# Rebuilt ends, and attention scores computed one slot ahead of their evacuation, in a top-k attention layer

## What is computed

```python
Q, K, V = proj(Wq, bq), proj(Wk, bk), proj(Wv, bv)        # B, H, L, D = 16, 16, 512, 16
scores = jnp.einsum('bhqd,bhkd->bhqk', Q, K) / math.sqrt(D)
top_vals, _ = jax.lax.top_k(scores, U)                    # U = 31
scores = jnp.where(scores < top_vals[..., -1:], -jnp.inf, scores)
context = softmax(scores) @ V
x = layernorm(x + context @ Wo.T + bo)
x = layernorm(x + (silu(x @ wg.T) * (x @ wu.T)) @ wd.T)
```

## Time and profile before

| | |
|---|---|
| median of 3 runs | 3061.3 us (3058.01 to 3065.76) |
| the profiled execution | 3046.8 us |
| its span | 3045.0 us |
| TensorE busy (PE) | 2680.3 us, 88% |
| VectorE, ScalarE, GpSimd busy (DVE, ACT, POOL) | 2481.3, 2480.9, 2407.2 us |
| granted TensorE clock, mean | 0.951 of 2.4 GHz |
| chain that ended last: PE, DVE, issue, SP's queue, POOL | 36%, 19%, 14%, 11%, 10% |

### The profile page before, as it was taken

How to read it: one execution, slowest core, us unless ns; L and a number is a source line. 1 busy time by engine, 2 the same in 40 slices (tenths; PEclk the granted TensorE clock), 3 DMA queues, 4 the chain that set the end, 5 groups by cost and what they waited for, 6 DMA issues and landing times.

```text
span 3045.0 us, 81353 instructions
## 1 busy us (share of the span) xinstructions
PE 2680.3 (88%) x21045; PEld 1454.1 (48%) x21375; DVE 2481.3 (81%) x12298; ACT 2480.9 (81%) x5894; POOL 2407.2 (79%) x1677
## 2 busy tenths in 40 slices
PE   5889989989998988889989999988989898899985
PEld 2444544545454444444545454444545454454443
DVE  4888888888888878888888888878888888888831
ACT  3788889888888977798888889978879887888931
POOL 1787988888888877788888889877869887888861
PEclk7889999999999999999999999999999999999976
DMA  2211111020111101011020111102011110202000
GB/s 81 48 25 38 28 39 39 25 47 26 41 25 40 39 22 43 18 41 39 25 46 25 43 23 44 36 25 46 26 36 30 34 43 19 47 20 50 2 15 7
DMA packets 91147, 102.67 MB, mean 34 GB/s; under 512 B 34514, under 2 KB 52947, under 8 KB 90579
## 3 DMA queue, kind: packets, MB, share of 16 engines
q1 hardware_dynamic: 88544, 93.73, 12.9%
q10 hardware_dynamic: 2034, 2.76, 0.3%
HBM read 20.86 MB, written 8.39 MB: 10 GB/s over the span
## 4 chain that ended last, share of the span: by engine, by line
PE 36%; DVE 19%; issue 14%; SPq 11%; POOL 10%; ACT 6%; DMA 2%; DVEq 1%; ACTq 0%; POOLq 0%
POOL mask L1070 8%; DVE cand L843 7%; PE bench L679 6%; SPq L349 6%; SPq L348 5%; PE Y_ps L608 5%; PE bench L673 4%; PE ST_ps L623 3%; DVE S L836 3%; PE Y_ps L606 3%; PE ctxT_ps L637 3%; PE bench L549 3%; PE ST_ps L620 2%; PE Y_ps L605 2%; ACT above L467 2%
## 5 line engine op out<-in xcount | busy, mean ns | idle before, releaser
L1070 POOL TENSOR_SCALAR mask<-S,thr,mb 128x512 bf16<-128x512 f32 x1024 | 2119.6, 2083 | 44.1 <-POOL mb L1064 30.0
L843 DVE MAX8 cand<-Y_ps 128x8 f32<-128x128 f32 x4096 | 1072.5, 282 | 5.3 <-issue 5.3
L457 ACT ACTIVATE junk<-S,at_zero,slope 128x512 bf16<-128x512 f32 x1024 | 824.6, 805 | 89.6 <-DVE S L836 89.5
L836 DVE TENSOR_SCALAR_CACHE_REDUCE S<-S_ps,na 128x512 f32<-128x512 f32 x1024 | 756.0, 738 | 163.2 <-PE S_ps L595 145.8
L467 ACT ACTIVATE above<-S,s,steep 128x512 bf16<-128x512 f32 x1024 | 824.5, 805 | 0.6
L475 ACT ACTIVATE PT<-ST_ps 128x512 f32<-128x512 f32 x1024 | 596.7, 583 | 205.7 <-PE ST_ps L623 200.2
L595 PE MATMUL S_ps<-KS,QS 64*128 64x512 f32 x1024 | 520.3, 508 | 4.2 <-DVE S L836 3.6
L608 PE MATMUL Y_ps<-KS,QS 64*128 64x512 f32 x1024 | 520.2, 508 | 0.0
L606 PE MATMUL Y_ps<-above,nbig 128*128 128x512 bf16 x1024 | 398.3, 389 | 85.4 <-DVE cand L843 57.4
L620 PE MATMUL ST_ps<-QS,KS 64*128 64x512 f32 x1024 | 415.4, 406 | 6.2 <-POOL mask L1070 6.2
L623 PEld LDWEIGHTS ST_ps<-nbig,mask 128*128 128x128 bf16 x4096 | 236.7, 99 | 382.5 <-issue 382.5
(11 more groups left out here) (125 smaller groups left out, 3682.1 us busy)
## 6 DMA issues: line engine op xcount, KB each, us to landing
QS<-Qhi SPq DMA_DIRECT2D x512, 32.0 KB, 2.0
KS<-Khi SPq DMA_DIRECT2D x512, 32.0 KB, 2.0
KS<-Klo SPq DMA_DIRECT2D x512, 32.0 KB, 2.0
QS<-Qlo SPq DMA_DIRECT2D x512, 32.0 KB, 2.0
xTs<-in_xT SPq DMA_DIRECT2D x17, 512.0 KB, 3.7
xs<-in_x SPq DMA_DIRECT2D x16, 512.0 KB, 3.9
out<-xs SPq DMA_DIRECT2D x16, 512.0 KB, 3.0
hT<-in_wgT ACTq DMA_DIRECT2D x1, 768.0 KB
```

The costliest lines, as they stand in the source:

```text
L457: nc.scalar.activation(junk[:, :], S[:, score_place(j)[0], :], ACT.Tanh, bias=at_zero[:, :], scale=slope[:, hb, col:col + 1], accum_out=s0 ...
L836: nc.vector.tensor_scalar(S[:, at, :], S_ps[n % 2][:, :], na[:, hb, col:col + 1], None, ALU.add, op1=ALU.max, accum_out=rmax[:, n % RING:n ...
L843: mx = nc.vector.max(cand[:, j % CANDS, i, :], Y_ps[j % 2][:, i * BW:(i + 1) * BW])
L1070: nc.gpsimd.tensor_scalar(mask[:, h % MASKS, t, :], S[:, score_place(j)[0], :], thr[:, r:r + 1], mb[:, r:r + 1], ALU.is_lt, op1=ALU.add).t ...
```

## The change

It has four parts. (1) The start: the network's weights are loaded by SP after the stacks of heads 0 and 1 (five DMAs) instead of by ScalarE's queue at the very start; q, k, keys, gram, quad and sums of the prologue go to six different banks, with semaphores of their own, and wait for fewer loads; ScalarE runs one tiny activation early. (2) TensorE computes the scores of tile T+1 in slot T, still before `turned`; S_ps keeps its two banks, so the wait is now for the evacuation of tile T-1. TensorE's loop holds seven batches (1 to 14) instead of five, and batch 15 stands behind it. (3) In the draining round VectorE makes every second one of the last 17 masks (`late_mask`), POOL the others. (4) The output projection, norms and network of batch 15 leave the draining round and follow it, each step with two banks or more, the copies shared by ScalarE and VectorE, the down-projection interleaved with gate and up over four banks, the last rows normalised on two engines and stored in two halves. The other functions take their bank and semaphores as arguments.

```diff
+LAST_TURN = (GROUP - 16) % TILES
...
-    if not first:
+    if not first and not rest:
...
+            def load_network():
+                sp.dma_start(wo[:, :, :], woT.rearrange("(c p) n -> p c n", p=P)).then_inc(ffn_loaded, 16)
+                sp.dma_start(brow, bo.rearrange("(a n) -> a n", a=1)).then_inc(ffn_loaded, 16)
...
+                sp.dma_start(wd[:, :, :].bitcast(I32), wdT.rearrange("(c p) n -> p c n", p=P)).then_inc(ffn_loaded, 16)
...
+            sp.dma_start(wqk[0][:, :, :], wqT.rearrange("(c p) n -> p c n", p=P)).then_inc(wq_loaded, 16)
+            sp.dma_start(wqk[1][:, :, :], wkT.rearrange("(c p) n -> p c n", p=P)).then_inc(w_loaded, 16)
+            sp.dma_start(wv[:, :, :], wvT.rearrange("(c p) n -> p c n", p=P)).then_inc(late_loaded, 16)
+            sp.dma_start(ranks[:, :], ranks_in).then_inc(late_loaded, 16)
+            sp.dma_start(bvc[:, :], bv).then_inc(late_loaded, 16)
+            sp.wait_ge(first_lo, 2)
             for h in range(HALF):
                 stack(h)
+                if h == 1:
+                    load_network()
...
+            rows = out[B - 1].rearrange("(n p) d -> p n d", p=P)
+            sp.wait_ge(out_done, (B - 1) * NT + 2)
+            sp.dma_start(rows[:, 0:2, :], xs[:, 0:2, :]).then_inc(stored, 16)
+            sp.wait_ge(last_rows, 4)
+            sp.dma_start(rows[:, 2:4, :], xs[:, 2:4, :]).then_inc(stored, 16)
+            sp.wait_ge(stored, 16 * (B + 2))
...
+            for w, src in ((0, bq), (1, bk)):
+                act.dma_start(bqk[w][:, :], src).then_inc(w_loaded, 16)
...
+            act.wait_ge(zero_set, 1)
+            nc.scalar.activation(junk[:, 0:1], at_zero[:, :], ACT.Identity)
             act.wait_ge(w_loaded, 16 * N_W)
...
             slots(0, True, False, False)
...
+            act.wait_ge(last_made, 1)
+            nc.scalar.activation(ctxT[:, :, 0:2 * P].rearrange("p c (n t) -> p n c t", n=2),
+                                 S_ps[0][:, :].rearrange("p (n c t) -> p n c t", n=2, c=C), ACT.Copy).then_inc(last_ctx[0], 1)
+            normalised(B, 0, (0, 1), x1_done)
+            for i in range(2):
...
+            for f in range(NF):
+                gate, up = PAIRS[f % 2]
+                act.wait_ge(last_gate, f + 1)
+                if f > 1:
+                    act.wait_ge(h_done, (B - 1) * NF + f - 1)
+                nc.scalar.activation(th[:, f % 2, :], gate[:, :], ACT.Tanh, scale=0.5 * DEQ).then_inc(th_done, 1)
+                act.wait_ge(last_up, f + 1)
+                if f:
+                    act.wait_ge(h_done, (B - 1) * NF + f)
+                nc.scalar.activation(ups[:, :], up[:, :], ACT.Copy, scale=0.5 * DEQ * DEQ).then_inc(last_ups, 1)
+            normalised(B, 1, (0, 1), out_done)
...
-                    if not rest:
-                        scores(T, n, b, first)
+                    if not rest and n + 1 < TILES:
+                        scores(T + 1, n + 1, b, first)
+                    if not rest and n + 1 == TILES and not last:
+                        scores(T + 1, 0, b + 1, False)
...
+            pe.wait_ge(wq_loaded, 16)
+            project(0, 0, Y_ps[0]).then_inc(first_made, 1)
+            pe.wait_ge(w_loaded, 16 * N_W)
+            project(1, 0, Y_ps[1]).then_inc(first_made, 1)
             pe.wait_ge(consts_done, 1)
+            pe.wait_ge(hi_done, 2)
+            keys(ST_ps[0]).then_inc(first_made, 1)
+            pe.wait_ge(first_keys, 1)
+            gram_matrix(ST_ps[1]).then_inc(first_made, 1)
+            pe.wait_ge(first_gram, 1)
+            quadratic(bench).then_inc(first_made, 1)
+            pe.wait_ge(first_quad, 1)
+            row_sums(ctxT_ps).then_inc(first_made, 1)
+            pe.wait_ge(late_loaded, 16 * N_LATE)
             pe.wait_ge(pool_consts, 1)
...
+            scores(0, 0, 0, True)
...
+            with pe.Fori(1, B - 1, PE_TURN_OF) as b:
+                for i in range(PE_TURN_OF):
                     slots(b + i, False, False)
+            slots(B - 1, False, False, True)
             slots(B, False, True)
+            pe.wait_ge(taken, place(B, LAST_TURN, "turn", 0, False, True) + 1)
+            for i in range(2):
+                turn_rows(lambda a, c: ctxs[:, 2 * i + a, c * P // D:(c + 1) * P // D, :].rearrange("p h d -> p (h d)"),
+                          S_ps[i]).then_inc(last_made, 1)
+            for i in range(2):
+                pe.wait_ge(last_ctx[i], 1)
+                project_out(i, Y_ps[i]).then_inc(last_made, 1)
+            for i in range(2):
+                if i == 0:
+                    pe.wait_ge(x1_done, (B - 1) * NT + 2)
+                else:
+                    pe.wait_ge(last_rows, 2)
+                turn_rows(lambda a, c: xs[:, 2 * i + a, c * P:(c + 1) * P], S_ps[i]).then_inc(last_made, 1)
+            def narrow_last(f):
+                pe.wait_ge(h_done, (B - 1) * NF + f + 1)
+                for t in range(NT):
+                    mm = nc.tensor.matmul(LAST_DOWN[t][:, 0:DM], hT[:, f, t * P:(t + 1) * P], wd[:, f, :],
+                                          start=(f == 0), stop=(f == NF - 1))
+                    if f == NF - 1:
+                        mm.then_inc(last_down, 1)
+            pe.wait_ge(last_split, 2)
+            for f in range(NF):
+                gate, up = PAIRS[f % 2]
+                if f > 1:
+                    pe.wait_ge(last_gated, f - 1)
+                widen(wg, f, gate).then_inc(last_gate, 1)
+                if f > 1:
+                    pe.wait_ge(last_ups, f - 1)
+                widen(wu, f, up).then_inc(last_up, 1)
+                if f > 1:
+                    narrow_last(f - 2)
+            narrow_last(NF - 2)
+            narrow_last(NF - 1)
...
+            def late_mask(b, T, n):
+                j = (n - MASK) % TILES
+                h, t, r = j // NT, j % NT, j % RING
+                wait_apart(dve, st_done, T - t - MASK - (MASKS - 1) * NT)
+                wait_apart(dve, mb_done, 2 * (b * NP + (n - MASK) // PAIR) + 2)
+                nc.vector.tensor_scalar(mask[:, h % MASKS, t, :], S[:, score_place(j)[0], :], thr[:, r:r + 1], mb[:, r:r + 1],
+                                        ALU.is_lt, op1=ALU.add).then_inc(mask_late, 1)
...
+                    if rest and n < MASK and (n - MASK) % 2:
+                        late_mask(b, T, n)
...
+            dve.wait_ge(last_made, 2)
+            nc.vector.tensor_copy(ctxT[:, :, 2 * P:4 * P].rearrange("p c (n t) -> p n c t", n=2),
+                                  S_ps[1][:, :].rearrange("p (n c t) -> p n c t", n=2, c=C)).then_inc(last_ctx[1], 1)
...
+            def normalised(i):
+                wait_apart(dve, mrstd_done, (B - 1) * 4 + 2 * i + 2)
+                for t in (2, 3):
+                    nc.vector.tensor_scalar(xs[:, t, :], xs[:, t, :], rstd[:, t:t + 1], shift[:, t:t + 1], ALU.mult,
+                                            op1=ALU.add).then_inc(last_rows, 1)
+            normalised(0)
...
+            for t in range(NT):
+                dve.wait_ge(last_down, t + 1)
+                nc.vector.tensor_tensor(xs[:, t, :], LAST_DOWN[t][:, 0:DM], xs[:, t, :], ALU.add).then_inc(last_sum, 1)
+                row_statistics(B, 1, (t,), last_sum, 3 + t)
+            normalised(1)
...
-                    if due(MASK, n, first, rest):
+                    if due(MASK, n, first, rest) and not (rest and (n - MASK) % 2):
...
+            layer_norm(B, 0)
+            for f in range(NF):
+                pool.wait_ge(last_gated, f + 1)
+                pool.wait_ge(last_ups, f + 1)
+                nc.gpsimd.tensor_tensor(hT[:, f, :], th[:, f % 2, :], ups[:, :], ALU.mult).then_inc(h_done, 1)
+            layer_norm(B, 1)
...
```

More of the change, by code:

```diff
@@ L523, in slots @@
                         count_first(T, n, b, first)
-                    if not first and n in X1_SLOTS:
+                    if not first and not rest and n in X1_SLOTS:
                         normalised(b, 0, X1_SLOTS[n], x1_done)
@@ L609, in below, with turned @@
                                  tile_position=(rows.start, 0)).then_inc(below_done, 1)
-            def turned(T, n, first):
+            def turned(T, n, first, rest):
                 j = (n - TURNED) % TILES
@@ L721, in on_bench, with slots @@
                     mm.then_inc(ready, 1)
-            def slots(b, first, rest):
+            def slots(b, first, rest, last=False):
                 for n in range(TILES):
@@ L776, in mark, with split_low @@
                 return steps[0]
-            def split_low(what, hb, splits, use):
-                dve.wait_ge(ready, use + 1)
+            def split_low(what, hb, splits, at, free):
+                bank, made, m = at
+                dve.wait_ge(made, m)
                 dve.wait_ge(hi_done, splits)
@@ L787, in head_gram @@
[L787 to L796 removed]
+                                               op0=ALU.add, op1=ALU.subtract).then_inc(free, 1)
@@ L808, in moments @@
+                    dve.wait_ge(free, f)
                     dve.nop(nofuse=True)
```

(18 more changed lines are left out.)

246 lines of the change are left out of this document (131 added, 115 removed).

## The result

The changed kernel takes 3048.8 us (median of seven runs, 3037.1 to 3060.6) against 3061.3 before: ratio 0.9956, interval 0.9935 to 0.9977. That is 12.5 us faster where 28 were forecast. The seven runs scatter by 24 us, mostly along with TensorE's granted clock, which is 0.950 of full speed in the fastest and 0.940 in the slowest. The profiled execution took 3044.3 us (span 3042.5), 4.5 under its median, where the one before lay 14.5 under its own; so the two profiles differ by only 2.5 us.

A forecast was written before the change was run, and what follows sets the result against it. TensorE was taken to set the pace within a batch, and engines taking turns to bound both ends. -9.0 - 19.5 - 6.5 - 26.5 + 34 = -27.5, say -28, from 3061.3 gives 3033 us timed; range 2988 to 3070.

The forecast's parts named there:

- the scores ahead, +34: Fifteen batches: scores computed a slot early cost 1.5 + 1.35 - 0.6 = 2.25 us a batch, 34 in all.
- the term for slot 59: Slot 59: TensorE waits for VectorE's evacuation behind the moments, 1.67 us later; taken as 1.5 a batch.
- Start, -9.0: Kernel start: Klo 11.5 us earlier, less 2.5 for five network loads put among the stacks' 64 DMA issues.
- Masks -19.5: Last masks, shared by POOL and VectorE: 16 us saved, and TensorE's clock stays up; -19.5 together.
- Context to x1T -6.5: Last context to x1T, 23.86 us: two banks a step let engines overlap; between 4.5 and 8.5 saved, 6.5 taken.
- Network 27: Batch 15's network: 53.44 us falls to 27, TensorE alone left and its clock rising in the first third; -26.5.
- rival B: Tail: the clock stays low, so masks give -4 instead of -19.5; -12 in all, 3049 us; chance 0.22.
- The same wait arises in slots 23 to 25 and 58: Slots 23 to 25 and 58: the evacuation wait replaces an equally long wait for maxima; cost nothing.
- I take 0.6: Gain where VectorE, no longer waiting for scores, stops holding TensorE; at most 0.6 us a batch.
- +0.33 in 16 slots: Every fourth slot: scores, below and L620 share one half of the array; +0.33 each, 1.35 a batch counted.
- Rival A: Batches: the scores ahead cost nothing net, slack and VectorE's lead cover them; -62, 2999 us; chance 0.22.
- Rival C: Batches: lost pairing paid in all sixteen slots, 7.0 a batch; slower, +43, 3104 us; chance 0.15.

The follow-up runs named there:

- e7: The change with the scores back in their own slot and all late masks back on GpSimd; 3010.0 us, 20.6 over the same kernel with shared masks.
- e8: The change with six unused matmuls put ahead of TensorE's wait for the evacuation in slots 24 and 59; 3023.2 us, ratio 0.989.
- e13: The change with moments in seven parts, flags copied before the exponential and xT loaded ahead of the last two stacks; 2924.6 us, ratio 0.957.
- e12: The change with scores back in their own slot, moments in seven parts and xT loaded ahead of the last two stacks; 2911.4 us, ratio 0.953.

## Why the prediction was half right

The step that failed is the price of the scores ahead, +34; in it above all the term for slot 59, 1.5 a batch, which measured 2.9.

**Start, -9.0: right.** -8.7. Klo was made at 13.1, not 15.0, 13.4 earlier instead of 11.5. The 64 issues with the five loads between them took 3.7 us more than the 64 alone did before, not 2.5: the loads' own issues are 2.5 of it (23.27 to 25.78), and the issues behind them, the first two of 0.94 and 1.06 instead of 0.59, the rest. The two errors nearly cancel: that the sum is so close is luck.

**Masks, context and network, -52.5: right.** -55.3 measured. Masks -19.5 against 20.6 by e7. Context to x1T -6.5 against -8.7 (23.86 to 15.19). Network 27 against 25.5. The clock stayed up as the forecast had it: rival B (the clock low in the tail) did not occur, and e7 shows that it does with the old masks. GpSimd's masks beside VectorE's took 2.21 us each in the mean instead of 2.06: in each group of four one was long, 2.34 and 2.66, and the others took 2.07. VectorE's took 0.52 to 0.97. The Trainium skill (SBUF — State Buffer, Who interferes with whom) has the two engines block each other wholly on a shared port pair, if VectorE's instruction is in a two-port mode or reads two inputs from SBUF; no run here shows the mode. Of the 3 us that the prediction set against this, GpSimd lost 0.9.

**Scores a slot ahead, +34: the step that failed.** The mechanisms that it named were right: a stall in slot 59, a lost pairing, a gain for VectorE. One was missing, the clock that falls behind a stall. They measured +61.6 over fifteen batches, 4.1 a batch against 2.25. By the table, a batch is +0.15 by row 12, +0.2 from there to row 32, +0.3 to row 58, +2.9 to row 60 and +0.3 to row 64, 3.84 in all. Four terms were mis-sized.

- *"First, slot 59 ... I take 1.5."* The stall is that long (the scores are 1.70 late; with the clock held up, in e8, the slot loses 1.2 against before). In the change the slot loses 2.9, because the clock fell behind it. I had read the same thing in the earlier trace rows, an idle stretch and then 0.50, and used it for the tail only.
- *"The same wait arises in slots 23 to 25 and 58 ... in place of a wait for maxima as long: nothing."* The waits of slots 24 and 25 are indeed no longer than before (1.83 us against 2.54 in batch 9), but the clock is low behind them in every batch instead of every second one, and 1.1 us are lost from row 24 to row 26. By row 32 they are given back, since the kernel before waits for xT there. So "nothing" came out nearly right, by luck. That the kernel before already had this low clock in its batches I had not seen; the earlier trace rows are of the network's slots alone.
- *"I take 0.6"* for the gain. TensorE did gain 1.70 by slot 9, three times that, and had lost it by slot 12, most of it to a wait for ScalarE's copy of the flags in slot 9, 1.17 a batch and 18.0 us in all, where the kernel before has 1.9.
- *"+0.33 in 16 slots."* A fourth slot's row costs 0.25 (the third matmul starts 0.59 after the first, not 0.34), and in the changed kernel steps of that size stand in slots 27, 51 and 55, with larger ones in 11 and 63 that it may be part of. Once the stalls are gone (e13) it is paid in eight. The forecast's 1.35 a batch was too much.

Rival A (the scores cost nothing) was wrong: even without these stalls they cost 13 us. Rival C's sign, a batch over 180, came, and so did the 4.1 a batch from which it decides, but not by its mechanism, the pairing in every fourth slot, which is only a part. What no rival had is that a stall's length is not its price. That the change came out faster at all rests on the two ends, which the forecast had right.

Open: what makes the clock fall behind one stall of 1.2 to 1.4 us and not behind another. The kernel before kept 1.00 behind slot 59 in 13 of 14 batches.

## What to carry to other kernels

Price a stall on TensorE as its length plus what may follow it at half clock; in slot 59 that more than doubled it (1.2 to 2.9 us), and filling it with useless matmuls won 25 us though the stall stayed. Look at the same place in the kernel before first: it may have the low clock already. When an edit that plainly removes waits moves the time by nothing, look per slot for the place where the gain comes back: here one load stood behind 64 issues in SyncE's queue, and two edits worth 3 and 15 us alone were worth 78 together. And where one engine is moved ahead of another, look at what stands in front of the instruction that now releases it, not at how long the other engine used to wait.

## What was not expected of the hardware

- TensorE busy 1.77 of 3.20 us at the full clock was followed by 3.40 us at 0.56; with the same gap filled (2.98 of 3.20, e8) the clock stayed at 1.00. After e7's idle time for masks it stood at 0.50 through windows in which TensorE was busy 14.77 of 16 us.
- Three matmuls on 64 rows start at 0.00, 0.00 and 0.34 when the first two lie on different halves of the array's rows (e12, slot 31), and at 0.00, 0.35 and 0.59 when all three share one (e13).
- A DMA issue of a stack costs SyncE's queue 0.63 us, so 64 of them are 41 us in which nothing else on that queue starts.
